# Setup of a graph kernel: the first product two blocks to a bank, step words, field and cell table beside it

## What is computed

```python
edge_index = jnp.stack([src, dst])
h = jnp.maximum(_layernorm(x, axis=-1), 0.0)
x = x + relu(concat([h, segment_sum(h[src], dst), segment_sum(edge_attr, dst)]) @ W.T + b)
h = jnp.maximum(_layernorm(x, axis=-1), 0.0)
h1 = relu((segment_sum(h[src], dst) / deg) @ W1_l + b1 + h @ W1_r)
h2 = relu((segment_sum(h1[src], dst) / deg) @ W2_l + b2 + h1 @ W2_r)
x = x + h2
```

## Time and profile before

| | us |
|---|---|
| median of 3 runs | 2033.34 |
| lowest, highest | 2031.09, 2033.35 |
| span of the profiled execution | 1450.0 |
| median less this span | 583.3 |
| TensorE busy, share of the span | 1368.8, 94% |
| VectorE, ACT, GpSimd busy | 812.4, 490.1, 654.9 |

### The profile page before, as it was taken

One profiled execution on the slowest core, in us unless ns is written; L12 is line 12 of the kernel. 1 busy time (PEld: TensorE's weight loads), 2 busy tenths in 40 slices (PEclk: granted clock), 3 DMA queues, 4 the chain that ended last, 5 costly groups with the idle time before them and its releaser, 6 DMA issues.

```text
span 1450.0 us, 34753 instructions
## 1 busy us (share of the span) xinstructions
PE 1368.8 (94%) x12165; PEld 1235.0 (85%) x12166; DVE 812.4 (56%) x1837; ACT 490.1 (34%) x1389; POOL 654.9 (45%) x772
## 2 busy tenths in 40 slices
PE   3777999999999999998999999999999999999996
PEld 3656999999999899997888888888888888888885
DVE  8686898888888888882454545432222222221221
ACT  2632123455688888882333232311111110000000
POOL 5400000011121121215777777167777745777775
PEclk9988999999999999999999999999999999999998
DMA  6108778888999988886565556566666665666663
GB/s 182 29 2 221 202 221 230 242 248 237 261 271 266 273 260 260 262 269 222 161 214 177 175 199 162 193 195 196 205 196 207 187 194 190 220 210 214 213 203 74
DMA packets 284762, 295.12 MB, mean 204 GB/s; under 512 B 19461, under 2 KB 250064, under 8 KB 284672
## 3 DMA queue, kind: packets, MB, share of 16 engines
q1 hardware_dynamic: 233861, 212.90, 46.9%
q0 software_dynamic: 26016, 69.24, 16.9%
q10 hardware_dynamic: 24795, 11.74, 2.8%
HBM read 245.70 MB, written 48.11 MB: 203 GB/s over the span
## 4 chain that ended last, share of the span: by engine, by line
PE 84%; POOL 2%; issue 2%; DMA 2%; ACT 2%; DVE 0%; ACTq 0%; POOLq 0%; DVEq 0%; SPq 0%
PE edge_banks L1065 41%; PE edge_banks L1023 20%; PE banks L997 10%; PE edge_banks L1096 4%; PE edge_banks L1019 4%; PE banks L1083 3%; POOL shared L833 2%; ACT shared L1252 1%; DMA shared<-in_edge_attr 1%; PE edge_banks L1072 1%; PE banks L1077 1%; ACT banks L1247 0%; DMA shared<-g_rows,list_src 0%; DMA shared<-counts 0%; ACT shared L1229 0%
## 5 line engine op out<-in xcount | busy, mean ns | idle before, releaser
L833 POOL DMA_INDIRECT shared<-g_rows,list_src x555 | 541.9, 976 | 230.8 <-issue 167.2
L1065 PE MATMUL edge_banks<-g_even,shared 128*128 128x257 f16 (+1 forms) x3822 | 444.7, 273 | 4.4 <-DMA shared<-counts 4.4
L1065 PEld LDWEIGHTS edge_banks<-g_even,shared 128*128 128x128 fp8e3 x3822 | 372.4, 97 | 62.6 <-issue 4.6
L1023 PE MATMUL edge_banks<-shared 128*128 128x128 f32 x2744 | 345.3, 277 | 4.4 <-issue 4.0
L1023 PEld LDWEIGHTS edge_banks<-shared 128*128 128x128 f32 x2744 | 325.8, 193 | 7.6 <-issue 7.0
L812 POOL DMA_DIRECT2D counts<-shared x156 | 76.4, 490 | 487.8 <-ACT shared L1252 472.8
L1639 DVE SCALAR_TENSOR_TENSOR shared<-edge_banks,shared,own 128x128 f32<-128x128 f32 x98 | 34.3, 350 | 367.6 <-PE edge_banks L1065 339.4
L1065 PE MATMUL edge_banks<-shared 128*128 128x256 f16 x1911 | 225.8, 272 | 0.2 <-DVE own L1621 0.2
L1551 DVE TENSOR_TENSOR shared<-iota,shared 128x3528 f16<-128x3528 f16 x98 | 195.5, 1995 | 51.2 <-PE banks L997 50.8
L1252 ACT ACTIVATE shared<-banks 128x392 uint16<-128x392 f32 x312 | 152.2, 488 | 184.6 <-PE banks L997 174.2
L1065 PEld LDWEIGHTS edge_banks<-shared 128*128 128x128 fp8e3 x1911 | 185.3, 97 | 30.7 <-DVE own L1621 0.5
(11 more groups left out here) (278 smaller groups left out, 997.6 us busy)
## 6 DMA issues: line engine op xcount, KB each, us to landing
shared<-in_edge_attr SPq DMA_DIRECT2D x195, 512.0 KB, 4.5
shared<-counts SPq DMA_DIRECT2D x117, 784.0 KB, 5.2
counts<-shared POOLq DMA_DIRECT2D x156, 196.0 KB, 3.8
shared<-g_rows,list_src POOLq DMA_INDIRECT x555
shared<-hot_rows SPq DMA_DIRECT2D x20, 304.0 KB, 2.9
g_rows<-g_even SPq DMA_DIRECT2D x1, 3136.0 KB, 15.5
g_rows<-shared ACTq DMA_DIRECT2D x49, 64.0 KB
g_rows<-g_even ACTq DMA_DIRECT2D x49, 64.0 KB
```

What stands on the lines that cost most here:

```text
L833: pool.indirect_dma_start(ring_g[use % RING][:, t, 0:2 * D], None, g_rows[r], bass.IndirectOffsetOnAxis(ap=list_src[:, at:at + 1], axis=0) ...
L1023: mm = pe.matmul(edge_wide[bank][:, :, at], ring[:, bank * GROUP_TILES + j, :], hot_dst[u][:, k, (j - 1) * SPREAD:j * SPREAD].unsqueeze(1) ...
L1065: mm = pe.matmul(acc[s][:, 0:wide], stream8[slot][:, order[h], :], G[r % 2][:, order[h], 0:wide], start=h == 0, stop=h == BLOCKS - 1, skip ...
```

## The change

It puts both blocks of a pair into one bank, so that four pairs can be in flight, and waits for the pair eight blocks back. ACT norms six turns ahead, and from turn 7 on it copies the high halves of both pairs. The step words are made in turns 1 and 2 with f16 operands, in four chunks of 504 steps, each copied by itself; the second row consists only of the two columns used of each nine. The list starts move from turn 1 to turn 4, the checks' sum from turn 9 to 6. The field is made behind pair 34 and turned in turns 10 and 11 into `flat[0]` and `flat[1]`; ACT copies all four pieces. The cell table is made behind pair 44, its doubling comes ahead of the turned lists. The diff, with most unchanged lines left out:

```diff
@@ -289,8 +289,8 @@
         off_i = small[:, 384:384 + SBLK].bitcast(I32)
-        off_f = small[:, 400:400 + SBLK]
-        w_next = small[:, 416:416 + SBLK]
+        off16 = small[:, 400:416].bitcast(F16)[:, 0:SBLK]
+        next16 = small[:, 416:432].bitcast(F16)[:, 0:SBLK]
@@ -583,15 +583,29 @@
         ROUNDS = 3
-        LIST_UP_AT, CHECKS_AT, OUTSIDE_AT, FIELD_AT, FLAG_AT = 2, 16, 36, 42, 46
-        AHEAD = 4
+        LIST_UP_AT, CHECKS_AT, FLAG_AT, FIELD_AT, CELL_AT = 12, 16, 28, 34, 44
+        LISTS_TURN, VIOL_TURN, FIELD_TURNS = 4, 6, (10, 11)
+        AHEAD, BOTH_FROM = 6, 7
+        NINES = 56
...
         NEW_TURN, NEW_DENSE = (34, 12), 6
-        WORDS = 6
+        WORDS = 8
...
         SCHUNKS = -(-SBLK // 4)
+        ROW_CHUNK = NINES * HALF
+        ROW_CHUNKS = -(-NSTEP // ROW_CHUNK)
+        BY_ACT = [b for b, n in PAIRS if b % 4 == 0 or b // 4 >= BOTH_FROM]
+
+        def pair_of(b):
+            return banks[:, b // 2 % BANKS, :].rearrange("p (n c) -> p n c", c=2 * D)
+
+        def row_bank(c):
+            return (banks[0:1, 2, :], banks[0:1, 3, :], flat[0][0:1, :], flat[1][0:1, :])[c]
+
+        def ends_in(lo, hi):
+            return [(b, max(lo, b * P), min(hi, (b + 1) * P)) for b in range(SBLK) if b * P < hi and (b + 1) * P > lo]
@@ -890,9 +904,11 @@
                 for b in range(b0, b1_):
-                    if b >= 4:
-                        pe.wait_ge(S["g0_taken"], (b - 4) // 2 * 2 + 2)
-                    pe.matmul(banks[:, b % 4, 0:2 * D], hT0[t % 2][:, (b - b0) * P:(b - b0 + 1) * P], w_l0[:, 0:2, :].rearrange("p k f -> p (k f)"),
+                    if b >= 2 * BANKS:
+                        pe.wait_ge(S["g0_taken"], (b - 2 * BANKS) // 2 * 2 + 2)
+                    if b == 4:
+                        pe.wait_ge(S["words_taken"], 5)
+                    pe.matmul(pair_of(b)[:, b % 2, :], hT0[t % 2][:, (b - b0) * P:(b - b0 + 1) * P], w_l0[:, 0:2, :].rearrange("p k f -> p (k f)"),
@@ -921,6 +937,28 @@
                 if t == 1:
+                    for j in range(PER):
+                        at, odd = (PER // 2 + j // 2, 1) if j % 2 == 0 else (j // 2, 0)
+                        mm = pe.matmul(flat[1][96:97, at:at + PER * (HOLDERS // 2 - 1) + 1:PER], c_end[:, j:j + 1],
+                                       identz[0:HOLDERS, 1 + odd:HOLDERS + odd:2], start=True, stop=True, skip_group_check=True)
+                    mm.then_inc(S["rows_up"], 1)
+                    pe.wait_ge(S["tables_ready"], 1)
+                    for c in range(ROW_CHUNKS):
+                        for b, lo, hi in ends_in(c * ROW_CHUNK, min((c + 1) * ROW_CHUNK, NSTEP)):
+                            mm = pe.matmul(row_bank(c)[:, lo - c * ROW_CHUNK:hi - c * ROW_CHUNK], off16[:, b:b + 1], ident16[:, lo - b * P:hi - b * P],
+                                           start=True, stop=True, skip_group_check=True)
+                        mm.then_inc(S["step_row_up"], 1)
+                if t == 2:
+                    pe.wait_ge(S["words_taken"], 6)
+                    for b in range(SBLK):
+                        for k, last in enumerate((PARTS[0][1] - 1, PARTS[1][1] - 1)):
+                            n0, n1 = -(-(b * P - last) // HALF), -(-(min((b + 1) * P, NSTEP) - last) // HALF)
+                            lo = n0 * HALF + last - b * P
+                            mm = pe.matmul(flat[0][0:1, 2 * n0 + k:2 * n1 + k - 1:2], next16[:, b:b + 1], ident16[:, lo:lo + (n1 - n0 - 1) * HALF + 1:HALF],
+                                           start=True, stop=True, skip_group_check=True)
+                    mm.then_inc(S["step_row_up"], 1)
+                if t == LISTS_TURN:
+                    pe.wait_ge(S["words_taken"], WORDS)
@@ -932,39 +970,27 @@
                     mm.then_inc(S["list_up"], 1)
-                    for j in range(PER):
-                        at, odd = (PER // 2 + j // 2, 1) if j % 2 == 0 else (j // 2, 0)
-                        mm = pe.matmul(flat[1][96:97, at:at + PER * (HOLDERS // 2 - 1) + 1:PER], c_end[:, j:j + 1],
-                                       identz[0:HOLDERS, 1 + odd:HOLDERS + odd:2], start=True, stop=True, skip_group_check=True)
-                    mm.then_inc(S["rows_up"], 1)
-                if t == 9:
+                if t == VIOL_TURN:
...
                     pe.matmul(flat[0][0:1, 80:85], ones[:, 0:1], viol, start=True, stop=True).then_inc(S["viol_up"], 1)
+                if t in FIELD_TURNS:
+                    pe.wait_ge(S["field_ready"], 1)
+                    for c in range(2):
+                        k = 2 * FIELD_TURNS.index(t) + c
+                        if k >= 2:
+                            pe.wait_ge(S["field_taken"], k - 1)
+                        for j in range(min(4, SBLK - 4 * k)):
+                            mm = pe.transpose(flat[c][:, j * P:(j + 1) * P], field[:, 4 * k + j, :], ident[:, :])
+                        mm.then_inc(S["field_up"], 1)
             dense(len(TURNS) - 1)
-            pe.wait_ge(S["g0_taken"], BLOCKS)
-
-            def step_row(col):
-                for b in range(SBLK):
-                    mm = pe.matmul(flat[b // 4][0:1, (b % 4) * P:(b % 4 + 1) * P], col[:, b:b + 1], ident[:, :], start=True, stop=True)
-                mm.then_inc(S["step_row_up"], 1)
-            pe.wait_ge(S["field_ready"], 1)
-            for c in range(SCHUNKS):
-                for j in range(min(4, SBLK - 4 * c)):
-                    mm = pe.transpose(banks[:, c, j * P:(j + 1) * P], field[:, 4 * c + j, :], ident[:, :])
-                mm.then_inc(S["field_up"], 1)
-            pe.wait_ge(S["tables_ready"], 1)
-            step_row(off_f)
-            pe.wait_ge(S["step_row_taken"], 1)
-            step_row(w_next)
             pe.wait_ge(S["list_field"], 1)
-            pe.wait_ge(S["step_row_taken"], 2)
+            pe.wait_ge(S["field_taken"], SCHUNKS)
...
 
-            pe.wait_ge(S["field_taken"], 2)
-            pe.wait_ge(S["cell_ready"], 1)
+            pe.wait_ge(S["g0_taken"], BLOCKS)
@@ -1171,6 +1197,7 @@
             quarts = words.rearrange("p a (q k) -> p a q k", k=QUART)
+            nines = words.rearrange("p a (q k) -> p (a q) k", k=QUART)
@@ -1185,11 +1212,11 @@
             def high(t):
-                b0, b1_ = TURNS[t]
-                n = min(2, b1_ - b0)
-                act.wait_ge(S["norms_ready"], 1)
-                act.wait_ge(S["g0_up"], b0 + n)
-                act.activation(G[0][:, b0:b0 + n, 0:D], banks[:, 0:n, 0:D], ACT.Copy, scale=up[:, 0:1]).then_inc(S["g0_high"], 1)
+                for b, n in PAIRS:
+                    if b // 4 == t and b in BY_ACT:
+                        act.wait_ge(S["norms_ready"], 1)
+                        act.wait_ge(S["g0_up"], b + n)
+                        act.activation(G[0][:, b:b + n, 0:D], pair_of(b)[:, 0:n, 0:D], ACT.Copy, scale=up[:, 0:1]).then_inc(S["g0_high"], 1)
@@ -1200,33 +1227,33 @@
                     turned(t - 1)
+                if t == 2:
+                    act.wait_ge(S["rows_up"], 3)
+                    act.activation(ends_row, flat[1][96:97, 0:NDUO], ACT.Copy).then_inc(S["words_taken"], 1)
+                    for c in range(ROW_CHUNKS):
+                        n = min(NINES, NSTEP // HALF - c * NINES)
+                        act.wait_ge(S["step_row_up"], c + 1)
+                        act.activation(nines[:, c * NINES:c * NINES + n, 0:HALF], row_bank(c)[:, 0:n * HALF].rearrange("p (a k) -> p a k", k=HALF), ACT.Copy
+                                       ).then_inc(S["words_taken"], 1)
+                if t == 3:
+                    act.wait_ge(S["step_row_up"], ROW_CHUNKS + 1)
+                    act.activation(nines[:, :, HALF:HALF + 2], flat[0][0:1, 0:2 * (NSTEP // HALF)].rearrange("p (a k) -> p a k", k=2), ACT.Copy
+                                   ).then_inc(S["words_taken"], 1)
...
                     normed(t + AHEAD)
+                if t in FIELD_TURNS:
+                    for k in (2 * FIELD_TURNS.index(t), 2 * FIELD_TURNS.index(t) + 1):
+                        act.wait_ge(S["field_up"], k + 1)
+                        n = min(512, SPAD - k * 512)
+                        act.activation(packed[:, k * 512:k * 512 + n], flat[k % 2][:, 0:n], ACT.Copy).then_inc(S["field_taken"], 1)
...
             high(len(TURNS) - 1)
-            for c in (1, 3):
-                act.wait_ge(S["field_up"], c + 1)
-                n = min(512, SPAD - c * 512)
-                act.activation(packed[:, c * 512:c * 512 + n], banks[:, c, 0:n], ACT.Copy).then_inc(S["field_taken"], 1)
-            act.wait_ge(S["rows_up"], 3)
-            act.activation(ends_row, flat[1][96:97, 0:NDUO], ACT.Copy).then_inc(S["words_taken"], 1)
-            steps = edge_banks[0:1, :, :].rearrange("p a c -> p (a c)")[:, 0:NSTEP].rearrange("p (a s) -> p a s", s=STEPS_ROW)
-            nines = steps.rearrange("p a (q k) -> p a q k", k=HALF)
-            act.wait_ge(S["step_row_up"], 1)
```

(41 more changed lines are left out.)

## The result

| us | before | after |
|---|---|---|
| median of 4 runs each | 2033.27 | 2020.39 |
| lowest, highest | 2031.09, 2033.35 | 2019.88, 2024.01 |
| span of the profiled execution | 1450.0 | 2018.4 |

The ratio is 0.9947, 95% interval 0.9933 to 0.9961: 12.9 us less (interval 7.9 to 13.6), where 5.3 were forecast. The sign is right and the size is not; the time lies outside the range of 2023.8 to 2032.3.

What follows compares the result with a forecast made beforehand. TensorE's chain bounds the kernel, so only the build's start, held up by the tail behind the product loop, counts. Loop 7.7 us longer, tail 12.3 shorter: 4.6 less, taken as 5.3, 2033.3 to 2028.0; range 2023.8 to 2032.3.

Steps and rivals of the forecast that it cites:

- Steps 1 and 2: Early product loop: norming further ahead loses 1.0 us; step words in turns 1 and 2 cost little, product 2 at 63.2.
- Step 3: Lists in turn 4 of the product loop: product 4 at 71.65, VectorE waits 2.6 us at pair 12.
- Step 4: Product loop from turn 7, ACT copying both high halves: a serial order of 3.1 us a turn, longer than 2.66.
- Step 5: Field in turns 10 and 11: TensorE waits 2.6 us for it; product 10 at 93.0, product 11 at 99.4.
- Step 6: Cell table behind pair 44: loop ends at 106.9 against 99.19, so it grows by 7.7 us.
- Step 7: Tail behind the loop: 5.6 us instead of 17.9, 12.3 saved; the cleared edge table stays hidden by 0.9.
- Rival D: Earlier build start not carried, as cleared table or zeroed banks bind or transfers run slower: gain 0 to 2; chance 0.08.
- the sum: First edge issue: loop end 106.9 plus tail 5.6 gives 112.5 against 117.10, 4.6 us less; 5.3 taken.
- A: Product loop: TensorE keeps 2.4 GHz from product 1 on, gain 7.7, up to 9.5 us; chance 0.20.
- B: Product loop: two more half-clock stretches, or step word matmuls at upper bounds, leave a gain of 2.5 us; chance 0.20.
- C: Product loop: waits nearly every turn hold TensorE at 1.2 GHz, issue 11 us later, 2044; chance 0.10 with lesser slips.

Runs made afterwards that it cites:

- k7: k2 with ACT copying the first pair's high half only, in all turns; 1438.81 us, ratio 0.9912 to before.
- k1: The kernel before with one more register operation ahead of each of two register waits; 1452.41 us, ratio 1.0003 to before.
- k5: k1 with TensorE's build loop put at a multiple of 256 instructions; 1448.99 us, ratio 0.9985 to before.
- k6: k2 with TensorE's build loop put at a multiple of 256 instructions; 1439.20 us, ratio 0.9923 to before.
- k10: k1 with TensorE's build loop 64 instructions past a multiple of 256, where before takes 2032.56; 2031.69 us, ratio 0.9994.
- k11: k2 with TensorE's build loop 64 instructions past a multiple of 256, where before takes 2032.56; 2022.22 us, ratio 0.9947.
- k4: k1 with TensorE's first matmul, of zeros, issued nine times instead of once; 1446.13 us, ratio 0.9971 to before.
- k2: The changed kernel with the same added register operations as k1; 1437.76 us, ratio 0.9904 to before.
- k9: The pairs alone, as k3, with TensorE's build loop at a multiple of 256 instructions, where before takes 2032.56; 2025.48 us, ratio 0.9966.
- k12: k8 with TensorE's build loop at a multiple of 256 instructions, where before takes 2032.56; 2017.71 us, ratio 0.9925.
- k3: k1 with only the pairs of the change: two blocks in one bank, four pairs in flight; 1445.64 us, ratio 0.9954 to before.
- k8: k2 with field and cell table back behind the loop and ACT copying first pairs' high halves only; 1433.62 us, ratio 0.9877 to before.

## Why the prediction was right and wrong

**Steps 1 and 2** held: product 0 at 52.1 (forecast 52.3), product 1 at 58.6 (58.5). Product 2 came 1.4 earlier, at 61.8: product 1 was laid out at 1.2 GHz (58.5 to 61.7) and ran at 2.4 in 1.97 us, and the 28 small matmuls took 0.90, not 1.15. **Step 3** held with that lead: product 4 at 70.1 (71.65), 6 at 76.3, 7 at 78.5 (77.0, 79.25), VectorE's wait behind pair 12 2.52 (2.6). **Step 4** was right in size, 3.1 us a turn, and k7 shows that it is worth nothing, because step 5 swallows it. **Step 5** held: a field wait of 2.36 (2.6), products 10 and 11 at 92.1 and 98.9 (93.0, 99.4). **Step 6**: loop end 105.74 (106.9). **Step 7**: tail 5.26 (5.6), cleared table done at 114.84, the first addition at 116.32. It stands 5.32 behind the issue, where the earlier trace rows have 4.09, so the clear is hidden by 1.5. What comes last there is the zeroing of the banks (L998), for which VectorE waits 1.80 us. Rival D named it; its price was not paid, since the 57th product stands 22.1 behind the issue as before.

The first issue is then at 111.00, laid out for 112.5. Against the trace of before that is 6.1 us less, against k1 6.8, where the sum said 4.6 and took 5.3. With the profiles at equal places (k5, k6) it is 9.8, with those of the second chip (k10, k11) 7.9. By terms of the sum: the tail saves 11.0, 12.5 and 13.2 us in these three pairs (forecast 12.3), and the loop grows by 4.3, 2.7 and 5.3 (forecast 7.7). **The growth of the loop is the mis-sized term.** A part of it lies in the kernel before, whose loop ends at 101.3 to 101.5 in k1, k4 and k5 and not at 99.19, behind the longer stretch at 1.2 GHz shown above; a part in the changed kernel, whose low stretches fall differently each time: k6 has full clock at 92 to 96 us, where k2 has half of it, and its product 11 is 2.2 earlier. The setup gain of the changed kernel is thus 7 to 10 us. The window of k2 and of k6 at the field (length, busy TensorE, granted clock, DMA share, GB/s):

```profile
92.00:94.00 2.00, 1.94 (x5) 0.50 0.00 0
94.00:96.00 2.00, 2.00 (x7) 0.50 0.00 0
```

```profile
92.00:94.00 2.00, 1.89 (x9) 1.00 0.00 0
94.00:96.00 2.00, 0.87 (x8) 1.00 0.00 0
```

**The step that failed** is the sentence that "the end moves by as much as the issue at 117.10 moves", written "nearly all of it behind the setup, in code that the change leaves alone". The code is unchanged, but its place in TensorE's stream is not. On the first chip the build of k2 is 4.7 us shorter than that of k1, 4.4 of it in the group behind the jump back, and the time moves by 13.9 where the first issue moves by 6.8; the pair k5, k6 with equal places shows both parts apart.

For the 12.9 us of the result the split is less sharp. About 8 come from the first issue (k10 to k11), against 5.3 in the sum, so the mis-sized loop is a large part of the miss. k11 takes 9.5 less than k10 and 10.3 less than before by the medians, and the interval of the result itself reaches down to 7.9. The remaining 3 to 5 us are in the build, in rounds that no profile of before on such a chip bounds, or in the spread of the runs: this stays open. The build of after is the shortest of all traces, 539.5.

**The second failed statement** is that 583.3 us "lie around it". They lie in it: in the runs timed, TensorE waits for "issue" in the rounds (1354 us against 785), and the first issue comes 14 to 17 us later (k9 to k12 against k3, k5, k2 and k8). It did little harm to the difference, since both kernels pay alike for the first issue (14.2 and 14.4 us, k5 to k10 and k2 to k11), but it was a wrong reading. A program whose span is two thirds of its median was not profiled under the conditions in which it was timed, and that could have been said before.

**The rivals.** A (more clock) gave 7.7 to 9.5, and of the measured setup gains 7.9 lies in that range and 9.8 just above it, but by luck: its condition, 2.4 GHz from product 1 on, was met in no trace. Of B the condition came and the price did not: k2 has half clock at 70 to 73, 90 to 97 and 104 to 111 us, more than the two stretches after 62 us that the prediction named as a sign of being wrong, but its first issue is earlier than forecast all the same. C did not happen, and D only as said at step 7: no ring at 1.2 GHz formed, although the waits of 0.68 in each turn were there; and the transfers followed the first issue (57th product 22.1 behind it in k2, 21.9 in before). None of the rivals had the place of the loop.

## What to carry to other kernels

Moving work from a tail into a loop pays only if the loop's engines don't wait for it: here the step words paid 4.5 us (k3 to k8), while the work that made TensorE and then the ring wait (field, cell table) cost 4.9 more than it saved (k8 to k7). When code ahead of a loop changes, look at the iteration behind the jump back before giving the gain to the edit; a variant with the loop at a fixed place tells the two apart, and the sum over all turns sizes it, not the median times the turns. And compare the span with the timed median first: where they differ by more than a few microseconds, the trace is of other conditions.
